# A graph network step on Trainium2: the messages of 22 of 125 target places summed from rows gathered per edge instead of by the dense product

## The reference

```python
def _step(embedding, src, dst, etype, W_msg, b_msg, w_ih, w_hh, b_ih, b_hh):
    n = embedding.shape[0]
    m = (embedding @ W_msg.T + b_msg).reshape(n, N_EDGE_TYPES, DIM)
    q = m[src, etype]
    r = jax.ops.segment_sum(q, dst, num_segments=n)
    return _gru_cell(r, embedding, w_ih, w_hh, b_ih, b_hh)
```

## Time and profile before

| | us |
|---|---|
| median of 3 runs | 2428.3 (2426.54 to 2430.07) |
| the profiled execution, its own time | 2424.79 |
| its span | 2423.3 |
| counting, 45 to 447 | 402 |
| hops, 469 to 1175 | 706 |
| a step | 310.7 |

### The profile page before, as it was taken

The page is one execution under the profiler, slowest core; times in us unless marked ns, Lnnn a source line. Parts: engine busy times, 40 slices in busy tenths (PEclk is TensorE's granted clock), DMA queues, the critical chain, the costliest instruction groups (busy, mean ns, idle before and its releaser), DMA issues.

```text
span 2423.3 us, 40583 instructions
## 1 busy us (share of the span) xinstructions
PE 2157.0 (89%) x14377; PEld 1404.1 (58%) x14888; DVE 1384.5 (57%) x2714; ACT 505.4 (21%) x1122; POOL 235.0 (10%) x517
## 2 busy tenths in 40 slices
PE   3555555599999999999999999999999999999998
PEld 2223223589998989889544565444654446544465
DVE  8878778687776767786822337323463224542243
ACT  4877778400000000000300103101021000210010
POOL 4645555000000000000000000000000000000000
PEclk9655556699999999999999999999999999999999
DMA  2000000100000000004100000000000000010000
GB/s 77 22 33 22 22 33 22 49 1 2 2 2 2 1 2 2 2 1 147 51 1 1 1 1 1 1 1 1 1 1 1 1 1 1 1 27 1 1 1 28
DMA packets 23056, 34.26 MB, mean 14 GB/s; under 512 B 2573, under 2 KB 18939, under 8 KB 22466
## 3 DMA queue, kind: packets, MB, share of 16 engines
q1 hardware_dynamic: 19897, 30.56, 3.8%
q10 hardware_dynamic: 2944, 0.93, 0.2%
HBM read 18.04 MB, written 13.45 MB: 13 GB/s over the span
## 4 chain that ended last, share of the span: by engine, by line
PE 77%; DVE 10%; ACT 7%; issue 4%; ACTq 1%; DVEq 1%; POOL 0%; DMA 0%; POOLq 0%
PE ps L819 43%; PE ps L898 26%; PE ps L802 4%; ACT weighed L538 3%; PE ps L786 2%; ACT packed L531 2%; ACT words L520 1%; ACTq L511 1%; DVE marks L1093 1%; DVE dig L1121 1%; DVE big L1123 1%; DVEq L1080 1%; PE ps L748 1%; PE ps L883 1%; DVE dig L1122 1%
## 5 line engine op out<-in xcount | busy, mean ns | idle before, releaser
L819 PE MATMUL ps<-slots,m_parts 125*128 125x500 fp8e4 (+1 forms) x5600 | 1083.3, 353 | 1.5 <-DVE slots L1398 1.0
L819 PEld LDWEIGHTS ps<-slots,m_parts 125*128 125x128 f16 x5600 | 546.3, 98 | 487.6
L898 PE MATMUL ps<-parts,big 125*128 125x256 f16 x6125 | 669.5, 273 | 6.8 <-issue 3.9
L898 PEld LDWEIGHTS ps<-parts,big 125*128 125x128 fp8e4 x6125 | 591.3, 98 | 63.5
L1398 DVE TENSOR_SCALAR slots<-big 128x3200 int32<-128x3200 int32 (+1 forms) x112 | 244.2, 2183 | 281.6 <-PE ps L819 281.6
L704 PE MATMUL ps<-hot_pair,weighed 125*128 125x228 f16 x1000 | 207.8, 354 | 182.6 <-DVE hot_pair L1095 102.4
L704 PEld LDWEIGHTS ps<-hot_pair,weighed 125*128 125x128 f16 x1000 | 111.9, 118 | 278.6 <-ACT weighed L538 242.1
L538 ACT ACTIVATE weighed<-marks,win_w 125x128 f16<-125x128 f16 x625 | 195.5, 389 | 90.1 <-DVE marks L1093 89.1
L1526 DVE SCALAR_TENSOR_TENSOR r_parts<-ps,over,r_parts 128x500 f16<-128x500 f32 (+1 forms) x28 | 19.1, 684 | 229.6 <-ACT r_parts L615 229.6
L477 ACT ACTIVATE rs<-rs 125x25 f32<-125x25 f32 (+3 forms) x5 | 1.1, 216 | 711.0 <-DVE rs L971 711.0
L1533 DVE SCALAR_TENSOR_TENSOR gate_r<-ps,over,gate_r 128x500 f32<-128x500 f32 (+1 forms) x28 | 19.1, 682 | 226.6 <-PE ps L802 226.6
(11 more groups left out here) (204 smaller groups left out, 1327.8 us busy)
## 6 DMA issues: line engine op xcount, KB each, us to landing
packed_counts<-packed SPq DMA_DIRECT2D x16, 625.0 KB, 2.9
big<-packed_counts SPq DMA_DIRECT2D x4, 1600.0 KB, 7.5
big<-packed_counts SPq DMA_DIRECT2D x3, 1200.0 KB, 6.4
hd<-in_x SPq DMA_DIRECT2D x1, 1562.5 KB
x_again<-in_x SPq DMA_DIRECT2D x1, 1562.5 KB
big<-x_after_hops SPq DMA_DIRECT2D x1, 1400.0 KB
x_after_hops<-x SPq DMA_DIRECT2D x4, 224.0 KB
out<-big SPq DMA_DIRECT2D x4, 224.0 KB
```

The lines of the kernel that those rows point to most:

```text
L819: last = pe.matmul(ps[:, k % 2, 0:SIZES[k] * Q], m_parts[0:Q, a, h, t * F:(t + 1) * F], slots_f8[0:Q, t % 2, 0:SIZES[k], a, 0:Q], start=a ...
L898: last = pe.matmul(ps[:, n % RING, 0:2 * F], tot_f8[0:Q, c, a, :], both((parts0, parts1)[par], a), start=a == 0, stop=a == TILES - 1)
```

## The change

103 of the 125 target places stay in the dense product. The other 22 (103 to 124) are "picked": their sums are made from rows that an indirect DMA gathers, one row per edge.

- After the messages of a step SyncE stores `m_parts` to a DRAM table `m_dram` with a row of 2 x 128 f16 (512 bytes) for each node and type, in five pieces of five tiles. All of it (6.4 MB) has to be there before the first gather.
- The 22 places make 11 pairs. A pair has a window of `GW = 15` chunks of 125 edges; GpSimd issues one indirect DMA per chunk (125 rows of 512 bytes), 15 a pair, 165 a step, 660 in all. The rows land in a ring of two pairs (`picked`), and a pair's gathers wait until TensorE has used the pair two before.
- TensorE sums a pair with `picked_rows`: 15 chunks x 2 parts = 30 products with 50 moving columns (the one-hot `hot_to` of the edges' targets: 2 places x 25 tiles), the gathered rows being the weights. The pairs stand between the types of blocks 1 to 5.
- A step has nine turns instead of seven: two "picked" turns (300 and 250 nodes) get gates and a cell of their own.
- The messages of the next step wait for the second picked turn, since it holds places of all tiles.
- At the start GpSimd, TensorE and ScalarE make two more edge tables (row index 4 x source + type, and target), VectorE the windows of the pairs and the one-hot `hot_to`; an input in which a pair needs more than 15 chunks goes the general way of the kernel.
- At the end of the last step all seven blocks are turned and added after block 6.

```diff
+QD = 103
+GW = 15
+ORDER = [("dense", 0), ("dense", 1), ("dense", 2), ("dense", 3), ("picked", 0),
+         ("dense", 4), ("dense", 5), ("picked", 1), ("dense", 6)]
+PAIR_AT = {(1, 0): 0, (1, 2): 1, (2, 0): 2, (2, 1): 3, (2, 3): 4, (3, 1): 5, (3, 3): 6, (4, 1): 7, (4, 3): 8, (5, 1): 9, (5, 3): 10}
...
@@ SyncE
+                with sp.Fori(0, STEPS) as s:
+                    for first, last in STORED:
+                        sp.wait_ge(s_mp, TILES * s + last + 1)
+                        for lo, hi in ((0, ROWS_A), (ROWS_A, Q)):
+                            sp.dma_start(m_dram.rearrange("(p a t) f -> p a (t f)", a=TILES, t=TYPES)[lo:hi, first:last, :],
+                                         m_parts[lo:hi, first:last, :, :, :].rearrange("p a t h f -> p a (t h f)")).then_inc(s_mst, 16)
@@ GpSimd, at the start
+            pool.tensor_scalar(edge_g[0:ROWS, 0, :], edge_i[0:ROWS, 1, :], float(TYPES), None, ALU.mult).then_inc(s_grow4, 1)
+            pool.tensor_copy(edge_g[0:ROWS, 1, :], edge_i[0:ROWS, 2, :]).then_inc(s_grow4, 1)
...
+            pool.tensor_tensor(edge_g[0:ROWS, 0, :], edge_g[0:ROWS, 0, :], edge_g[0:ROWS, 1, :], ALU.add).then_inc(s_grow, 1)
...
+            pool.tensor_copy(edge_g[0:ROWS, 1, :], edge_i[0:ROWS, 0, :]).then_inc(s_grow, 1)
@@ GpSimd, in the steps
+                for s in range(STEPS):
+                    pool.wait_ge(s_mst, 16 * 2 * len(STORED) * (s + 1))
+                    for pair in range(PAIRS):
+                        r = pair % 2
+                        pool.wait_ge(s_got_used[r], USES[r] * s + pair // 2 + 1)
+                        for w in range(GW):
+                            at = pair * GW + w
+                            pool.indirect_dma_start(
+                                out=picked[0:CH, r, w, :, :].rearrange("p h f -> p (h f)"), out_offset=None, in_=m_dram[:, :],
+                                in_offset=bass.IndirectOffsetOnAxis(ap=edge_row[0:CH, at:at + 1], axis=0)).then_inc(s_got[r], 16)
@@ TensorE
-                        last = pe.matmul(ps[:, k % 2, 0:SIZES[k] * Q], m_parts[0:Q, a, h, t * F:(t + 1) * F],
-                                         slots_f8[0:Q, t % 2, 0:SIZES[k], a, 0:Q],
+                        last = pe.matmul(ps[:, k % 2, 0:SIZES[k] * QD], m_parts[0:Q, a, t, h, :],
+                                         slots_f8[0:Q, t % 2, 0:SIZES[k], a, 0:QD],
...
+            def picked_rows(s, pair):
+
+                r, at = pair % 2, pair % HALF * PC
+                pe.wait_ge(s_sel, 1)
+                wait_alone(s_got[r], 16 * GW * USES[r] * s + 16 * GW * (pair // 2 + 1))
+                for w in range(GW):
+                    for h in range(2):
+                        last = pe.matmul(ps[:, 6 + pair // HALF, at:at + PC], picked[0:CH, r, w, h, :], hot_to_f8[0:CH, pair, w, :],
+                                         start=w == 0 and h == 0, stop=w == GW - 1 and h == 1, skip_group_check=True)
+                last.then_inc(s_got_used[r], 1)
...
+                        if t == 1 and k and ORDER[TURN_OF["dense", k] - 1][0] == "picked":
+                            turn_gates(*ORDER[TURN_OF["dense", k] - 1])
+                        if (k, t) in PAIR_AT:
+                            picked_rows(s, PAIR_AT[k, t])
@@ VectorE
+            dve.wait_ge(s_to, PAIRS)
+            TT(hot_to[0:CH, :, :, :].rearrange("p g w n -> p (g w) n"),
+               iota_to[0:CH, :].rearrange("p (o n) -> p o n", o=1).broadcast_to([CH, PAIRS * GW, PC]),
+               win_to[0:CH, :].rearrange("p (m o) -> p m o", o=1).broadcast_to([CH, PAIRS * GW, PC]), ALU.is_equal).then_inc(s_sel, 1)
```

More of the change, by code:

```diff
@@ L692, in _ @@
             pe.sem_inc(s_hot_used, DEPTH)
+            for r in range(2):
+                pe.sem_inc(s_got_used[r], 1)
             pe.sem_inc(s_hot_used_g, W)
@@ L789, in message_when_ready @@
             def message_when_ready(s, a):
[L790 removed]
+                whole = max(TURN_OF["picked", 1], TURN_OF["dense", BLOCK_OF[a]])
+                pe.wait_ge(s_el, TURNS * s + whole + 1 - (TURNS - BLOCKS))
                 message(s, a)
@@ L1600, in gnn_step @@
-                if more_steps:
-                    for a in range(2, AHEAD):
-                        low(s + 1, a)
-                    dve.wait_ge(s_eh, BLOCKS * (s + 2))
-                    emb_low(START[BLOCKS - 1], SIZES[BLOCKS - 1])
-                else:
-                    add_results((5, 6))
+                for u, (what, i) in enumerate(ORDER):
+                    turn, n = TURNS * s + u, turn_size(what, i)
+                    tiles, places = turn_places(what, i)
+                    last, meanwhile = u == TURNS - 1, None
+                    after = ORDER[u + 1] if not last else None
+                    if what == "dense":
+                        if not last:
+                            unpack(s, i + 1, 0)
+                        elif more_steps:
+                            unpack(s, BLOCKS, 0)
+                        sum_low(turn, ps[:, i % 2, 0:n], r_parts[:, u % 2, 1, 0:n], r_parts[:, u % 2, 0, 0:n])
+                        if not last:
+                            if after[0] == "picked":
+                                sum_low(turn + 1, picked_sums(after[1]), picked_parts(after[1], u + 1, 1), picked_parts(after[1], u + 1, 0))
+                            unpack(s, i + 1, 1)
+                            meanwhile = lambda: unpack(s, i + 1, 2)
+                        elif more_steps:
+                            unpack(s, BLOCKS, 1)
+                            messages(s + 1, 0, 2)
+                            meanwhile = next_bias
+                        else:
+                            add_results((0, 1))
+                            meanwhile = lambda: add_results((2,))
+                    update(step, turn, n, emb[:, tiles, places],
+                           lambda m: m[:, 0:n].rearrange("p (c q) -> p c q", q=places.stop - places.start), meanwhile)
+                    dve.sem_inc(s_emb, 1)
+                    if what == "dense" and not last:
+                        unpack(s, i + 1, 3)
+                    if more_steps:
+                        if last:
+                            for a in range(2, AHEAD):
+                                low(s + 1, a)
+                        dve.wait_ge(s_eh, TURNS * s + BLOCKS + u + 1)
+                        emb_low(tiles, places)
@@ L1608, in _ @@
+                if not more_steps:
+                    add_results((3, 4, 5, 6))
             with dve.If(over_any < 1):
```

288 lines of the change are left out of this document (178 added, 110 removed).

## The result

The changed kernel takes **2577.5 us** (median of 4 runs, 2576.9 to 2578.4) against 2428.1 for the kernel before, measured beside it: ratio 1.062, interval 1.0603 to 1.0633. It is 149 us slower where 116 faster was forecast, and it lies 67 us above the range. The profiled execution's span is 2576.8 us.

The account below looks back on a forecast made before the run. In the four steps TensorE alone was taken as the bound. From the profiled 2424.8 us, -122 over four steps, +3 at the start and +3 at the end gave 2308.8, or 2312 us at the median; range 2285 to 2510.

Parts of the forecast that it names:

- What is G? ... I take 1.1: Gathers on GpSimd: 1.1 us from one to the next, so TensorE does not wait, which holds up to 1.2.
- G: Time from one gather to the next on GpSimd; above 1.2 us every 0.1 costs 16.5 us a step.
- nearest rows: Profile rows for the gather rate: ScalarE's queue issuing 512 pieces, 1.32 us; a small GpSimd operation beside VectorE, 1.06.
- Rival 2: In the steps GpSimd's gathers set the pace, above 1.376 us each, TensorE waiting before nearly each pair; 2510 at 1.5; chance 0.27.
- the rival's lock: Gathers beside VectorE's unpacking: descriptors can't be written in its two-port mode; up to 18 us a step, 0.11 a gather.
- Dense products, -45.8 us a step: TensorE's dense products in a step narrow to 412 and 309 columns, 175.9 and 132.5 ns each: -45.8 us.
- Message part, +1.5: In the message part VectorE takes the bound over at about 1.40 us a round: +1.5 us a step.
- Picked products, +13.6: TensorE's 330 picked products a step at 38 ns, with 11 empty loads: +13.6 us (10.0 to 16.9).
- Gates +0.2, cells and other waits nothing: Picked turns add 36 gate products, +0.2 us a step; their cells hide in idle time and next messages don't wait.
- Start, +3: At the start, GpSimd's four new operations, some 2.5 us each, and TensorE's turning of the new table: +3 us (0 to 8).
- End, +3: At the end VectorE adds four blocks behind the last cell instead of two, and the stores bunch: +3 us (1 to 6).
- Clock 1.00 throughout: Sign of a right forecast: TensorE's granted clock stays at 1.00, the 2.4 GHz level.

Follow-up runs that it names:

- experiment 2: The changed kernel with 64 rows a gather instead of 125, the number of gathers staying 660; 2378.6 us (one run).
- experiment 1: The changed kernel with 10 gathers for a pair instead of 15, all 30 products still done, some sums wrong; 2303.1 us.
- 9: The changed kernel with 15 picked places, single, 8 gathers each, instead of 22 in pairs, and VectorE making the edge rows at the start; 2340.6 us.

## Why the prediction was wrong

- **The step that failed** is "What is G? ... I take 1.1". G is 1.514 us bare (1.21 busy, 0.30 between) and 1.590 with the gathers lengthened beside VectorE. Given that number the forecast's own arithmetic comes out: 36.5 + 2 + 165 x 1.590 + 44.2 (behind pair 10) = 345.1 us, measured 345.4. Some of that is luck: the gathers started 38.9 us into the step instead of 36.5, and the part behind pair 10 took 41.9 instead of 44.2, which cancel. The last rows landed 3.8 us after the last issue, where the forecast has one G and 2 us, 3.6.
- **Why it was taken at 1.1.** Both "nearest rows" were of another kind: a hardware queue's issue of 512 pieces, and a tiny operation beside VectorE. They were treated as brackets of a value near the threshold of 1.2, though the rows' own bounds were 0.31 and 2.1 and the break-even was 1.376. An unknown multiplied by 660 on the path should have had its chance by its bounds: of the stretch from 0.31 to 2.1 a good 40% lies above 1.376, where 27% were given. And neither row holds a price per row, which is some 0.63 us of the 1.51 (experiment 2). The estimate by the Trainium skill's first byte of about 1 us (DMA: Bandwidth & Descriptors, Latency and other measured facts) is a latency and says nothing of the distance between two gathers, 1.51 us here.
- **Rival 2 is what happened**: its point (G above 1.376), its mechanism (TensorE waits on rows 41 times for 44 pairs) and its formula. By it G = 1.590 gives 2312 + 3.9 x 66 = 2569; the 8 us that are left are about what the start took over its +3. That the clock falls in the waits, which the rival counted against the change too, hardly reached the step. The range ended at G = 1.5 and was too short for its own unknown. Of the rival's lock, up to 0.11 us a gather was estimated; it is 0.076.
- **Dense products, -45.8 us a step:** right, 176.2 and 132.7 to 132.9 ns. Part of that is luck: an odd run counts as the next even one, so 103 columns of a tile are 104, and what was taken as 4 ns over the columns is some 3.
- **Message part, +1.5:** a round takes 1.41 us, VectorE's pace, as forecast (1.40).
- **Picked products, +13.6:** 25 ns each with 50 columns in experiment 1, and 24 ns with 25 columns in 9 (16 in 0.39 us), below the lower bound of 27; 38 was taken. The price does not follow the columns at this size. That, 330 x 13 ns = 4 us a step, is the difference between the forecast's 280.2 and the 276.35 of experiment 1, whose time, 2303.1, is 9 us under the forecast (16 less in the steps, 6 more at both ends). The Trainium skill (TensorE: Matmul & The Clock Gate, Back-to-back issue gap) gives 62 ns only with hardware decode off, and otherwise an issue floor of about 25 ns; the trace agrees with the latter, and the prediction left it out.
- **Gates +0.2, cells and other waits nothing:** right; in experiment 1 TensorE waits 2.5 us for the cell ahead of the next messages, as it did before (2.4).
- **Start, +3:** measured +10.6, above its bound of 8. GpSimd's took up to 4.30 us instead of 2.5, and beside them two operations of VectorE took 2.8 us more each and two more 1.0; `hot_to` was right (8.76 us for 9.0, and it fitted). The degree products took 1.4 us more. **End, +3:** measured +1.8.
- **Clock 1.00 throughout:** only where TensorE does not wait; in the steps of the changed kernel it is 0.91 to 0.92.

## What to carry to other kernels

Work that is moved to an idle engine has a rate there, and if the trace shows no operation of its kind, the price times the count must stand under the break-even with its upper bound, or the change has to be made smaller: here 120 gathers instead of 165 turn 6% slower into 3.4% faster. An indirect DMA from GpSimd in this kernel costs some 0.88 us and 5 ns a row, with 256 and 512 bytes a row alike, so few gathers with all partitions full are the cheap way. Where GpSimd becomes the bound, look at what VectorE runs beside it: a slower form of an operation there can make the kernel faster, but only where VectorE itself does not bound.

## What the runs showed of the hardware that was not expected

- An indirect DMA holds GpSimd for 1.21 us (125 rows) or 0.90 us (64 rows), and 0.30 us pass before the next; 256 or 512 bytes a row make no difference to it. Its rows land 3.3 us after the issue (2.9 with 256 bytes).
- A dense product whose moving operand has runs of an odd number of one-byte columns costs as much as with the next even number: 4 x 109 as 4 x 110 (18.63 us for 100), 3 x 109 as 3 x 110 (14.05), while 4 x 108 takes 18.30 and 3 x 108 13.80.
- The same unpacking runs at two rates by its shape, and the rate does not follow its size: 2600 elements in 1.50 us, 1950 in 2.18; 75 rows out of the 100 take 2.18 as well. The fast form is the one that holds up GpSimd.
- GpSimd and VectorE on 1375 elements each, side by side: 4.24 and 4.36 us, where VectorE's alone takes 1.59.
